# Keys and values of the third attention projected inside the routing stage of the first experts, and the stages around it regrouped

## The reference

```python
x = x + xattn_0(norm(x), ctx, mask)            # 16 heads of 16, a 0/1 mask on the scores
x = x + ffn_0(norm(x))                         # self-attention, layer norm, 1 of 4 experts, layer norm
x = x + xattn_1(norm(x), ctx, side, common)    # 16 heads, scores + 2*side + common term
x = x + ffn_1(norm(x))                         # 2 of 16 experts, and 2 shared ones
```

```python
ff = relu(x @ W1[e] + b1[e]) @ W2[e] + b2[e]
return layer_norm(x + ff) * ln2_g + ln2_b
```

## Time and profile before

| | us |
|---|---|
| median of 3 runs (1906.54 to 1913.85) | 1909.92 |
| the profiled execution's own time | 1910.97 |
| its span, first to last instruction | 1909.2 |
| PE busy (83%) | 1593.3 |
| DVE busy (58%) | 1108.6 |
| ACT busy (41%) | 790.3 |
| POOL busy (24%) | 465.4 |

### The profile page before, as it was taken

How to read it: one execution, slowest core, us unless ns; L and a number is a source line. 1 busy time by engine, 2 the same in 40 slices (tenths; PEclk the granted TensorE clock), 3 DMA queues, 4 the chain that set the end, 5 groups by cost and what they waited for, 6 DMA issues and landing times. The chain is left out here.

```text
span 1909.2 us, 24269 instructions
## 1 busy us (share of the span) xinstructions
PE 1593.3 (83%) x8256; PEld 1030.3 (54%) x8256; DVE 1108.6 (58%) x2704; ACT 790.3 (41%) x1248; POOL 465.4 (24%) x245
## 2 busy tenths in 40 slices
PE   6799999898999994399636499889988998899993
PEld 3466666654444433299514355555564556576772
DVE  6699999755676748022387588878753540122224
ACT  2388888421555561022103477768622121111110
POOL 0000000020000001311100799899533143111111
PEclk9899999987899997699868799999979999899997
DMA  7633433033223202666335798888333011644414
GB/s 264 204 100 100 118 96 89 1 143 100 63 73 82 68 23 78 222 212 191 114 127 228 268 304 298 283 295 280 134 150 116 1 43 60 206 157 152 146 61 146
DMA packets 136800, 276.56 MB, mean 145 GB/s; under 512 B 23792, under 2 KB 65904, under 8 KB 127088
## 3 DMA queue, kind: packets, MB, share of 16 engines
q1 hardware_dynamic: 129312, 258.98, 41.2%
q0 software_dynamic: 5264, 14.06, 2.0%
q10 hardware_dynamic: 2112, 2.10, 0.3%
HBM read 215.36 MB, written 59.69 MB: 144 GB/s over the span
## 5 line engine op out<-in xcount | busy, mean ns | idle before, releaser
L694 DVE CUSTOM_DVE_ANT_0 X<-pS,M 128x512 f32<-128x512 f32 x512 | 340.3, 690 | 80.1 <-POOL M L620 54.5
L634 PE MATMUL pS<-k,q 65*128 65x512 f32 (+1 forms) x512 | 255.4, 502 | 87.6 <-DVE mx L694 52.1
L620 POOL TENSOR_TENSOR M<-C,M 128x2048 f32<-128x2048 f32 x64 | 290.5, 4584 | 135.5 <-DMA M<-in_fside_Bx16xSxS 135.5
L643 PE MATMUL pT<-ident,X 128*128 128x128 f32 x2048 | 307.9, 274 | 0.3 <-ACT PT L730 0.3
L643 PEld LDWEIGHTS pT<-ident,X 128*128 128x128 f32 x2048 | 256.1, 141 | 40.2 <-issue 3.6
L877 DVE TENSOR_REDUCE nm<-pS 128x1 fp32r<-128x512 f32 x256 | 167.9, 687 | 80.9 <-PE pS L819 70.1
L634 PEld LDWEIGHTS pS<-k,q 65*128 65x128 f32 (+1 forms) x512 | 98.6, 193 | 212.9 <-DVE mx L694 125.2
L525 PE MATMUL pO<-PT,V 128*17 128x512 f32 x1536 | 205.5, 611 | 1.0 <-ACT OT L904 1.0
L722 ACT ACTIVATE X<-X,nm 128x512 f32<-128x512 f32 x256 | 164.0, 712 | 34.8 <-DVE nm L700 34.8
L722 ACT ACTIVATE X<-X,mx 128x512 f32<-128x512 f32 x256 | 164.7, 716 | 21.0 <-DVE mx L694 21.0
L707 DVE COPY PT<-pT 128x1024 f32<-128x1024 f32 x128 | 156.1, 1220 | 6.6 <-PE pT L643 6.6
(11 more groups left out here) (268 smaller groups left out, 2145.5 us busy)
## 6 DMA issues: line engine op xcount, KB each, us to landing
M<-in_fside_Bx16xSxS SPq DMA_DIRECT2D x64, 1024.0 KB, 7.3
w<-in_L_ffn_ew SPq DMA_DIRECT2D x48, 512.0 KB, 4.3
w<-in_L_ffn_W SPq DMA_DIRECT2D x23, 1024.0 KB, 5.4
q<-q_stacks SPq DMA_DIRECT2D x192, 64.0 KB, 3.2
k<-k_stacks SPq DMA_DIRECT2D x128, 64.0 KB, 3.0
M<-mask SPq DMA_DIRECT2D x16, 512.0 KB, 3.7
xs<-top_in SPq DMA_DIRECT2D x51, 128.5 KB, 5.1
k_stacks<-hi SPq DMA_DIRECT2D x24, 256.0 KB, 2.1
```

Of the source, the lines that this page charges most:

```text
L620: eng.tensor_tensor(M[:, slot], C[:, b % 2], M[:, slot], ALU.subtract).then_inc(s_m, 1)
L634: eng.matmul(pS[:, qt % 2, :], of, by, start=True, stop=True).then_inc(s_s, 1)
L643: ins = eng.transpose(pT[:, kt, qt * P:(qt + 1) * P], X[:, t % 3, qt, kt * P:(kt + 1) * P], self.ident[:])
L694: eng.tensor_tensor_reduce(X[:, i % 3, qt, :], pS[:, qt % 2, :], M[:, slot, qt, :], 2.0 if mask is None else 1.0, HIGHEST if mask is None ...
```

## The change

It regroups five pieces of work.

1. `com` is made in the first attention by POOL: SP loads fside_SxS2 and the padding row at head 4; POOL halves the matrix once (128x2048), and for each batch makes `low` (128x512) and adds the two (128x2048, two inputs in SBUF); SP stores the results at heads 15, 23, 31 and 39.
2. The second attention's `fetch` also loads the third attention's weights (six more transfers), and SP writes `blank` over `XS` there; POOL fills it at the start.
3. The second `output` carries loads in its SP queue: the context (2 MB), ln2's gain and shift, and the four W2 (4 MB).
4. `route_top1` also projects the third attention's keys and values: 8 groups of one key tile and two value tiles on PE, three of them ahead of the two routing matmuls. The value bias is a third matmul with one row of ones. ACT takes the tiles out, then rounds all keys to `hi`; DVE takes the rest at its own end; SP stores 16 tiles of 256 KB at the end. `top1_tiles` gets the whole second layer norm: add the tile's rows, statistics, square root on ACT, gain and shift, and only then the scatter.
5. `combine_top1` and the third `project` are gone; `queries` takes their place: read `YS`, add to x, normalise, turn, multiply by Wq, split, store. The one `recycle` between them becomes two: after the first `output`, and ahead of `queries`.

```diff
@@ attention_turned, sync, in the loop over heads i
+                        if per_group and i == 4:
+                            eng.dma_start(am[:], self.t["fside_SxS2_0"].rearrange("(p t) k -> p t k", p=P)).then_inc(s_am, 16)
+                            eng.dma_start(pad[:], self.t["mask_BxS2_bf0"].partition_broadcast(P)).then_inc(s_am, 16)
+                        if per_group and i % 8 == 7 and 1 <= i // 8 <= B:
+                            b = i // 8 - 1
+                            eng.wait_ge(s_com, b + 1)
+                            eng.dma_start(terms[b], com[:]).then_inc(s_cs, 16)
@@ attention_turned, gpsimd
+                        eng.tensor_scalar(am[:], am[:], -0.5, None, ALU.mult).then_inc(s_half, 1)
+                        for b in range(B):
+                            need(eng, s_com, b)
+                            eng.tensor_scalar(low[:], pad[:, b], 3.0e38, 10.0, ALU.mult, ALU.mult).then_inc(s_low, 1)
...
+                            need(eng, s_cs, 16 * b)
+                            eng.tensor_tensor(com[:], am[:], low[:].unsqueeze(1).to_broadcast([P, ST, S]), ALU.add).then_inc(s_com, 1)
@@ attention_direct, sync, at pair 16
                             fetch(eng)
+                            eng.wait_ge(s_id, 2)
+                            eng.dma_start(XS.rearrange("(p r) d -> p r d", p=P), blank[:]).then_inc(s_zero, 16)
@@ route_top1, sync, after the four load_expert
+                    for n in range(NK):
...
+                        for half, (s, buf) in enumerate(((s_hi, hi), (s_lo, keys))):
+                            eng.wait_ge(s, n + 1)
+                            eng.dma_start(KS[rows].rearrange("h d r s -> (h d) r s")[:, half], buf[:, n, :].bitcast(F32)).then_inc(s_ks, 16)
+                    eng.wait_ge(s_ks, 16 * 2 * NK)
@@ route_top1, scalar
+                    for n in range(NK):
+                        eng.wait_ge(s_pk, n + 1)
+                        eng.activation(keys[:, n, :].bitcast(F32), pj[:, n % 2, :], ACT.Identity, bias=...).then_inc(s_ke, 1)
+                        for v in (2 * n, 2 * n + 1):
...
+                            eng.copy(self.V[:, b * H:(b + 1) * H, j, 0:DK], pv[:, v % 2, 0:D]...).then_inc(s_ve, 1)
+                    for n in range(NK):
+                        eng.wait_ge(s_ke, n + 1)
+                        eng.copy(hi[:, n, :], keys[:, n, :].bitcast(F32)).then_inc(s_hi, 1)
@@ route_top1, tensor
+                    for n in range(3):
+                        key(n)
+                        value(2 * n)
+                        value(2 * n + 1)
                     eng.wait_ge(s_c, 5)
                     eng.wait_ge(s_oh, 1)
...
+                    for n in range(3, NK):
+                        key(n)
+                        value(2 * n)
+                        value(2 * n + 1)
                     eng.wait_ge(s_ix, 1)
                     self.expert_of_tile = [eng.value_load(...) for i in range(L0_TILES)]
@@ top1_tiles, vector, in the loop over tiles
                             eng.tensor_tensor(y, py[:, a % 2, 0:D], b2[:, a % 4, :], ALU.add).then_inc(s_yb, 1)
+                            eng.wait_ge(s_yb, a + 1)
+                            then(eng.tensor_tensor(y, y, x, ALU.add))
+                            then(eng.bn_stats(st[:, a % 2, :], y))
+                            then(eng.bn_aggr(mv[:, a % 2, :], st[:, a % 2, :]))
+                            eng.tensor_scalar(dev, mv[:, a % 2, 1:2], EPS, None, ALU.add).then_inc(s_var, 1)
                         if i < L0_TILES:
                             ... relu of the second half ...
+                        if i > 0:
+                            eng.wait_ge(s_dev, a + 1)
+                            then(eng.reciprocal(dev, dev))
+                            then(eng.scalar_tensor_tensor(out=y, in0=y, scalar=mv[:, a % 2, 0:1], in1=self.gain[:], op0=ALU.subtract, op1=ALU.mult))
+                            eng.scalar_tensor_tensor(out=y, in0=y, scalar=dev, in1=self.shift[:], op0=ALU.mult, op1=ALU.add).then_inc(s_yo, 1)
@@ queries (new), scalar and vector, in the loop over batches b
+                    for b in range(B):
+                        deviations(b)
+                        if b:
+                            split(b - 1)          # two of: Identity (whole), copy (hi, strided)
+                        for k in range(KD):
+                            n = b * KD + k
+                            eng.wait_ge(s_tr, n + 1)
+                            eng.copy(zT[:, k, b * S:(b + 1) * S], bank[:, n % 4, :]).then_inc(s_ev, 1)
+                    split(B - 1)
...
+                        for n in rows:
+                            eng.tensor_tensor(x[:, n, :], x[:, n, :], y[:, n, :], ALU.add).then_inc(s_a, 1)
...
+                        if b >= 2:
+                            rest(b - 2)           # two of: lo (strided)
+                        eng.wait_ge(s_dev, b + 1)
```

More of the change, by code:

```diff
@@ L479, in _ @@
                         need(eng, s_st[n % 4], stored[n % 4][n])
-                        eng.copy(hi[:, n % 4, :], rows_of(n)).then_inc(s_hi, 1)
+                        eng.copy(hi[:, n % 4, :], whole[:, n % 2, :]).then_inc(s_hi, 1)
                 @block.gpsimd
@@ L920, in output, with _ @@
             with nc.Block() as block:
+                if fetch is not None:
+                    @block.sync
+                    def _(eng):
+                        fetch(eng)
                 @block.tensor
@@ L1152, in expert_rows, with load_second @@
         self.s_we = [self.sem("s_we") for _ in range(4)]
+        self.gain, self.shift = (self.sb(n, [P, D], ctx=ctx) for n in ("gain", "shift"))
+    def load_second(self, eng, gain, shift):
+        for row, of in ((self.gain, gain), (self.shift, shift)):
+            eng.dma_start(row[:], of.partition_broadcast(P)).then_inc(self.s_w2, 16)
+        for e in range(E0):
+            eng.dma_start(self.w2[:, e], self.t["L0_ffn_W2"][e].rearrange("(m p) d -> p m d", p=P)).then_inc(self.s_w2, 16)
     def load_expert(self, eng, tile_expert, i):
@@ L1284, in _ @@
                         eng.dma_start(y[:, b * ST:(b + 1) * ST, :], YS[b * S:(b + 1) * S].rearrange("(t p) d -> p t d", p=P)).then_inc(s_g[b], 16)
-                    eng.dma_start(grow[:], gain.partition_broadcast(P)).then_inc(s_w, 16)
-                    eng.dma_start(brow[:], shift.partition_broadcast(P)).then_inc(s_w, 16)
-                def before(eng, chain, b):
-                    eng.wait_ge(s_g[b], 16)
-                    rows = slice(b * ST, (b + 1) * ST)
-                    chain(eng.tensor_tensor(y[:, rows], y[:, rows], xx[:, rows, 0:D], ALU.add))
-                    chain.wait()
@@ L1293, in combine_top1 @@
-                rs = self.normalise(block, s_ch, s_mv, s_rs, s_z, y, y, ctx, gain=grow, shift=brow, before=before,
-                                    ready=lambda eng: eng.wait_ge(s_w, 32))
+                    for n in range(NQ):
+                        c, m = divmod(n, KD)
+                        rows = slice(c * H + m * (P // DK), c * H + (m + 1) * (P // DK))
+                        for half, (s, buf) in enumerate(((s_hi, hi), (s_lo, lo))):
+                            eng.wait_ge(s, n + 1)
+                            eng.dma_start(QS[rows].rearrange("h d r s -> (h d) r s")[:, half], buf[:, n % 4, :].bitcast(F32)).then_inc(s_qs[n % 4], 16)
@@ L1296, in _, with deviations, split @@
                 @block.scalar
                 def _(eng):
-                    self.deviations(eng, s_mv, s_rs, rs)
+                    def deviations(b):
+                        rows = slice(b * ST, (b + 1) * ST)
+                        eng.wait_ge(s_var, b + 1)
+                        eng.activation(rs[:, rows], rs[:, rows], ACT.Sqrt).then_inc(s_dev, 1)
+                    def split(b):
+                        if b == 0:
+                            eng.wait_ge(s_sc, 1)
+                        for m in range(KD):
+                            n = b * KD + m
+                            eng.wait_ge(s_p, n + 1)
+                            need(eng, s_lo, n - 1)
+                            eng.activation(whole[:, n % 2, :], pj[:, n % 4, :], ACT.Identity, bias=scaled[:, m:m + 1], scale=q_scale).then_inc(s_t, 1)
+                            eng.wait_ge(s_t, n + 1)
+                            need(eng, s_qs[n % 4], 32 * (n // 4))
+                            eng.copy(hi[:, n % 4, :], by_blocks(n)).then_inc(s_hi, 1)
@@ L1303, in _, with rest @@
-                    eng.tensor_tensor(x[:], x[:], y[:], ALU.add)
+                    def rest(b):
+                        for m in range(KD):
+                            n = b * KD + m
+                            eng.wait_ge(s_hi, n + 1)
+                            need(eng, s_qs[n % 4], 32 * (n // 4))
+                            eng.tensor_tensor(lo[:, n % 4, :], by_blocks(n), hi[:, n % 4, :].bitcast(F32), ALU.subtract).then_inc(s_lo, 1)
```

(1 more changed line is left out.)

245 lines of the change are left out of this document (167 added, 78 removed).

## The result

| | before | changed |
|---|---|---|
| first comparison, median (lowest to highest) | 1910.43 us (1906.54 to 1913.85), 6 runs | 1896.11 us (1887.99 to 1899.55), 6 runs |
| second comparison (e9 below) | 1908.88 us, 7 runs | 1890.52 us (1882.58 to 1897.92), 4 runs |
| profiled execution, span | 1909.2 us | 1897.4 us |

The ratio is 0.9918 with a 95% interval of 0.9892 to 0.9945 in the first comparison and 0.9887 (0.9837 to 0.9936) in the second. The change gains 14 to 18 us where 32.5 were forecast.

What follows compares the result with a forecast made beforehand. Combine and project, a chain of DVE, ACT and transfers, lay wholly on the path: 108.85 us. -108.85 + 45.8 + 1.7 + 1.7 + 2.9 + 12.3 + 11 + 1 = -32.5, forecast 1878 us, range 1862 to 1895.

Steps and rivals of the forecast that it cites:

- the queries' stage: Stage replacing combine and project, from the first read of `YS` to the third attention's first load: 45.8 us.
- the routing matmuls slip: Routing: three groups ahead of them on PE, with the cold clock, move the routing matmuls 5.9 us later.
- the tail of the tiles with its `recycle`: Expert tiles' end: further passes and small steps before the last scatter, 2.9 us, plus the moved `recycle`, 1.7 us.
- The first output, with the other `recycle`: After the first `output`: the new `recycle` there adds 1.7 us.
- the second attention: Small maxima transfers queue behind `blank` on SP: between nothing and 8.4 us, taken as 1.
- The first attention: POOL's operations hold DVE's `nm`: four adds 10 us, halving and `low` about 1, so 11; bounds nothing and 20.
- The end of routing: 4 MB of stores at 335 GB/s take 12.5 us and end the stage, 12.3 us later; ends 7.6 and 17.
- no hold: Rival, first attention: `nm` runs through beside POOL, sum -43.5, 1867 us; chance 0.23.
- PE's clock would be low all through the queries' stage: Rival, queries or there and held stretches: stage 60 us against 45.8, +14, 1892 us; chance 0.17.
- The register reads: Routing's end: PE's 19 reads hide up to 0.75 us each; rival, reads or stores rule: +8, 1886 us, chance 0.06.
- The expert loop: Rival, expert tiles: the loop becomes DVE's or the store's, 15 tiles times 4 us, 1938 us; chance 0.04.
- The third attention hid nothing: Rival: the change moves work but the third attention's waiting transfers hide it, no change; chance 0.03.

Runs made afterwards that it cites:

- e9: The changed kernel once more, unedited: 1890.52 us, ratio 0.9887 to the kernel before.
- e3: Changed kernel with `blank` written in 19 transfers, one per pair from pair 6 on, instead of one at pair 16: 1886.1 us, ratio 0.9883.
- e4: Changed kernel with the six loads of the third attention's weights at pair 24 instead of pair 16, `blank` left whole at 16: 1884.79 us, one time.
- e1: Changed kernel with the first attention's 128x4 negation `nm` moved from DVE to ACT: 1867.21 us, ratio 0.9792.
- e5: Changed kernel with ACT rounding each key tile at once in routing, not all eight after the last eviction: 1885.42 us, ratio 0.9883.
- e8: Changed kernel without the sixteen stores of the third attention's keys (4 MB) and the wait for them: 1889.8 us, one time.
- e7: As e6, but one group of keys and values ahead of the routing matmuls, not three: 1859.73 us, ratio 0.9739.
- e6: Changed kernel with the edits of e1, e3, e4 and e5 together: 1859.85 us, ratio 0.9740.

## Why the prediction was wrong

**The shape of the sum was right.** What the change does beside the attentions was priced within 2 us a term: 46.5 us for the queries' stage (45.8); 5.9 us by which the routing matmuls slip (14.2 against 8.3, foretold 5.9), 14.2 us for routing (12.3), 3.2 for the tail of the tiles with its `recycle` (4.6). (The first output, with the other `recycle`, grew by 0.3 where 1.7 was added.) The tiles' period kept its length: 950 records of PE in 140.07 us against 140.03, with DVE's busy time up from 29.5 to 71.8 beside it. Each of these came from counting instructions along one chain.

**The term that failed is the second attention, +1 for what was 5.4 to 18.5 us in the six profiles that have the wait, 12 on average.** The prediction looked at what stands behind `blank` in SP's queue and found the two transfers of the maxima. It left out what stands there too, the six loads of a coming pair, for which PE has to wait once SP's lead is used up. Its upper bound, the 8.4 us of `blank`, did hold the wait itself, 5.4 to 7.6, but the value within the bounds was taken for the wrong transfer, and no bound had what comes behind the wait. e3 and e4 show that the wait shrinks to 0.5 us and 0.3 when either half of the cause goes. The rest of the 12 us is PE's clock. e9 shows that most of the changed kernel's 13 us of it can be missing from another execution; that a piece of 10 to 17 us at the lower clock follows every one of the six waits says that some of it belongs to the change. How much, these profiles do not settle.

**The first attention was right in mechanism and short in size.** The hold was forecast in 4 adds at 2.5 us and about 1 for the rest, 11. Measured: 12.9 of holds, as the halving of `am` takes POOL 5.39 us and not less than an add, and caught an `nm` for 3.62 by itself. On top come 5 us in which PE's clock was lower, which the prediction had only in its upper bound of 20. e1 shows both together: without the held instruction the stage loses 21 us, of which 3 are DVE's work moved to ACT, and the clock is back. The size is steady: the six kernels that keep the 128x4 form took 277.7 to 283.7 us for the stage. On its page "SBUF — State Buffer" (shared port pair) the Trainium skill has the loser wait for the winner's whole instruction, and the ends of the rows above agree with it to 0.04 us, at 128x4 as well, which the trace of before had left open.

**The end of routing was right for the right reason, by 2 us.** The prediction took 12.5 us for 4 MB of stores at 335 GB/s and let them end the stage, and in the changed kernel they do. e5 refutes the reading by ACT's order: start the stores sooner and they share the DMA engines with W1 and the scatters, and land hardly sooner. e8 removes them, and 7.7 us go. The next chain stands close behind: PE's projections with the register reads, 4.3 us ahead of the stores' landing in the changed kernel, ends the stage in e8 and in e7. That is why neither moving the groups (e7) nor leaving out the stores (e8) brings the stage below the kernel before's.

**The rivals.** That there would be no hold (1867 us) fell. That PE's clock would be low all through the queries' stage, 60 us, fell too: it was low in parts (0.76 on average) and the stage took 46.5. The register reads cost nothing in the changed kernel, as predicted, but not for the price that was set: at 0.86 us each they are above the 0.75 up to which they were to hide, and they hide because they begin 4.6 us before PE's last matmul ends and the stores take until 845.9. In e7 they are 5.0 us on the path. The expert loop did not become DVE's. The third attention hid nothing, for it starts 62 us sooner after the first read of `YS`. Its shared code was 5.1 us shorter in the changed kernel's profile; the part from POOL's first add there to the end took 845.1 us in the kernel before, 839.8 in the changed one and between 840.6 and 850.8 in the nine experiments, with no edit in it, so that is spread.

**The reckoning.** The profiled executions differ by 11.8 us where 32.5 were foretold, 20.7 less: 6.9 in the first attention, 17.5 in the second, 1.6 at its output, 1.9 in routing and 0.7 in the queries, together 28.6; less 1.4 at the first output, 1.4 in the tiles and 5.1 of spread in the shared code, which is 20.7. By the medians, 14 to 18 us, the shortfall is 14 to 18: 6.9 for the first attention, 5 for the wait in the second and 2 for routing are shown; the 0 to 4 that are left are no more than the clock behind the wait can account for, and within the spread of the medians. I had given the range from 1862 to 1895 and did not put the upper ends of the two attentions (20 and 8.4) together: 1878 + 9 + 7.4 = 1894.4, and with a routing tail at its upper end more, all from my own bounds.

## What to carry to other kernels

Work given to an idle engine or an idle queue is free only when nothing that the full engines need passes the same port or stands behind it in the same queue. List every instruction of DVE that has one SBUF tensor in and out, however small, before POOL gets a large one beside it; and list all that is issued behind a large transfer up to the point where the next consumer is due, not only what looks urgent. A stage that ends with a full set of DMA engines was hardly shortened by starting its transfers earlier; leaving bytes out of it did, down to the next chain. Look for that one before the edit: here it was PE's projections and 19 register reads, which no busy time shows.

## What the runs showed of the hardware that I had not expected

- A DVE instruction of 128x4 that usually takes 0.17 us was held for up to 4.08 us beside POOL (in e5); four of 128x1 in its place took 0.34 us in all, beside the same POOL instruction.
- POOL's halving, with one input of 128x2048, took 5.39 us; its add with two such inputs 4.54.
- A 2.4 MB transfer ahead of 128 KB loads in the same queue made them land after 9.0 and 9.4 us instead of 2.5 and 2.9.
- Reading one number into a register of PE took 0.68 to 0.70 us in the kernel before, e7 and e8, and 0.86 to 0.91 in the changed kernel, e5 and e6, where the reads lie beside more of the stores. Full DMA engines alone don't make the difference, for they were full in the kernel before too; what does was not tried.
- The same kernel's same 1006 PE records took 237.3 us in one execution and 225.2 in another, at a mean granted clock of 0.85 and 0.89. The Trainium skill's page "TensorE: Matmul & The Clock Gate" (Part 1) says of the slow matmuls with which a kernel starts that their number varies from run to run; these are in the middle of a stage, and there the slow pieces vary too. One profile of each kernel can't settle a question of 12 us in such a stage, and the medians of four to seven runs here moved by 5.6 us between two comparisons of the same kernel.
